# A transpose on TensorE that takes over the last addition of GpSimd

## The chip, the cores and the metric

The kernel runs on one core of a Trainium2 chip. Its engines work side by side, each through its own list of instructions, and wait for each other by semaphores: TensorE (PE; its weight loads are a row of their own, PEld), VectorE (DVE), ScalarE (ACT), GpSimd (POOL) and SyncE (SP), which starts transfers. The metric is the device time of one execution in microseconds, as the median over several.

## The reference

A GRU runs over 32 time steps on 32 sequences of 256 features; its states go through a feed-forward layer with a router, and the result is added to the input.

```python
def cell(h, x):                                   # 32 steps, one after the other
    gi = x @ W_ih + b_ih;  gh = h @ W_hh + b_hh   # [32, 768] each
    r = sigmoid(i_r + h_r);  z = sigmoid(i_z + h_z)
    n = tanh(i_n + r * h_n)
    h_new = (1.0 - z) * n + z * h

probs = softmax(xt @ w_router)                    # 1024 tokens, 128 experts
topk_p, topk_idx = top_k(probs, 4)
basis = silu(xt @ w_gate) * (xt @ w_up)           # [tokens, K=8, I=128]
mixed = einsum('tek,tki->tei', mix[topk_idx], basis)
out   = einsum('teh,te->th', mixed @ w_down, topk_w * expert_scale[topk_idx])
shared = silu(xt @ shared_w_gate) * (xt @ shared_w_up) @ shared_w_down
return x + out + shared
```

The kernel computes the routed part as one vector of 8 coefficients per token: the 8 basis blocks of 128 columns are scaled by them and added up to one block, which then goes through w_down.

## The kernel before, in words

The 1024 tokens are 8 chunks of 4 time steps by 32 sequences, 128 tokens each, one to a partition. Everything runs in the order in which it is written, engine by engine; no scheduler changes it.

**The recurrence.** In step t TensorE multiplies the state by W_hh (h_part, L619: 8 products of 32-column blocks of the array, which leave 16 records), ScalarE and VectorE apply the gates, and VectorE turns the new state (hT, L886). While they do so TensorE computes the input part of the next step (x_part, L583, 16 records) and then a piece of feed-forward work of a chunk that is complete: the filler. Before each filler piece stands what the order in filler(f) says, with k the step within a chunk, six steps behind the recurrence.

**The feed-forward work of chunk p.** k = 0: logits and unit 0 (a unit is 256 columns of gate and of up, each product of a token block by a weight in three reduced-precision parts, L640). k = 1: units 1 and 2, and project(p - 2). k = 2: the transpose of the expert mask (turn_em, L675), unit 3, and the coefficients (L681). k = 3: turn_hidden(p - 1) (L690 to L692), and unit 4. ScalarE and VectorE turn each unit into q, the basis, or shared.

**GpSimd.** In every step it first splits the new state into a high and a low part (halves: hThi L304, hTlo L306), for which it waits for hT. Behind that it does one piece of mixing: for k = 3 and k = 0 the scaling of q by the coefficients (qc, L316, 512 columns each), for k = 1 the addition of the two halves (half, L323), for k = 2 add_rest: 512 columns to 256 (quarter, L327), then 256 to 128 (mixed, L332). The semaphore pool_mix counts these operations, MIX_STEPS a chunk.

**The turn.** turn_hidden waits for pool_mix to reach the end of the chunk, and transposes mixed and the two blocks of shared into the bank turned, with ident as the moving operand. ScalarE (dhi, L485) and VectorE (dlo, L982) split it, and project (L702) multiplies by w_down two steps later.

**The tail.** After the last recurrent step the same work of the last chunks goes on without gate products, in an order of its own. The last chunk is scaled by ScalarE before it is added, so GpSimd only makes quarter from it (L380, L384); last_mixed_turned (L727) adds two parts of quarter and two blocks of q by four products with ident that accumulate in one bank. turn_hidden is so called seven times: for chunks 0 to 4 in the middle of the kernel, for chunk 5 in the tail's first part, for chunk 6 (LAST - 1) among the last chunk's units.

Of the kernel before, what the change touches and what calls it, by code (L numbers as in the profile page):

```python
# [29 lines left out]
ALU = mybir.AluOpType  # L30
# [3 lines left out]
P = 128  # L34
# [6 lines left out]
E, K, I = 128, 8, 128  # L41
# [19 lines left out]
def build(nc, x, cond, w_ih, w_hh, b_ih, b_hh, w_router, w_gate, w_up, w_down, amplitudes, expert_scale,  # L61
          sw_gate, sw_up, sw_down, out):
    with ExitStack() as ctx:
        def sb(name, shape, dt=F32):
            return ctx.enter_context(nc.sbuf_tensor(name, shape, dt))

        def bank(name):
            return ctx.enter_context(nc.psum_tensor(name, [P, 512], F32))

        def sem(name):  # L70
            return ctx.enter_context(nc.semaphore(name))
# [19 lines left out]
        ident = sb("ident", [P, P])  # L91
# [41 lines left out]
        qc = sb("qc", [P, K * I])  # L133
        half = sb("half", [P, 4 * I])
        quarter = sb("quarter", [P, 2 * I])
        mixed = sb("mixed", [P, I])
        dhi = sb("dhi", [P, 2, 3, P], F32R)
        dlo = sb("dlo", [P, 2, 3, P], F32R)
        ot = sb("ot", [P, 2, D])
# [4 lines left out]
        turned = bank("turned")  # L144
# [64 lines left out]
        pool_mix = sem("pool_mix")  # L209
        turned_ready = sem("turned_ready")  # L210
# [6 lines left out]
        stored = [sem("stored0"), sem("stored1")]  # L217

        TOPK_STEPS = 2
        MIX_STEPS = 5  # L220

        PIECES = [(u, s) for u in range(NU) for s in range(KB)]
        LO_VECTOR = sum(LO_VECTOR_AT, [])
# [1 line left out]
        LAST = NC - 1  # L225
# [59 lines left out]
        @block.gpsimd  # L285
        def _(pool):
            pool.wait_ge(zeroed, 2)
            pool.affine_select(out=pick4[:, :, :], in_=pick4[:, :, :], compare_op=ALU.not_equal, fill=1.0,
                               base=0, pattern=[[-1, NJ], [0, Q]], channel_multiplier=1).then_inc(const_ready, 1)
            pool.affine_select(out=ident[:, :], in_=ident[:, :], compare_op=ALU.not_equal, fill=1.0,  # L290
                               base=0, pattern=[[-1, P]], channel_multiplier=1).then_inc(const_ready, 1)
            pool.wait_ge(bias_ready, 1)
            pool.tensor_copy(early[:, :, HN:HN + FJ],
                             bias[:, HN:HN + FJ].rearrange("p (o c) -> p o c", o=1).to_broadcast([P, NE, FJ]))\
                .then_inc(early_hn, 1)

            def halves(t):

                c, k = t // TC, t % TC
                pool.wait_ge(hT_ready, t + 2)  # L300
                if k == 0 and c >= 3:

                    pool.wait_ge(unit_ready, NU * (c - 2))
                pool.tensor_copy(hThi[:, c % 3, :, :, k], hT[:, c % 2, :, k, :]).then_inc(hThi_ready, 1)  # L304
                pool.wait_ge(hThi_ready, t + 1)
                pool.tensor_tensor(hTlo[:, c % 3, :, :, k], hT[:, c % 2, :, k, :],  # L306
                                   hThi[:, c % 3, :, :, k].bitcast(F32), ALU.subtract).then_inc(hTlo_ready, 1)


            def scale_basis(p, part):  # L310

                if part == 0:
                    pool.wait_ge(coef_ready, p + 1)
                pool.wait_ge(q_ready, NU * p + 2 * (part + 1))
                ks, cols = slice(K // 2 * part, K // 2 * (part + 1)), slice(K // 2 * I * part, K // 2 * I * (part + 1))
                pool.tensor_tensor(qc[:, cols].rearrange("p (k i) -> p k i", i=I),  # L316
                                   q[:, p % 2, cols].rearrange("p (k i) -> p k i", i=I),
                                   coef[:, p % 2, ks].rearrange("p (k o) -> p k o", o=1).to_broadcast([P, K // 2, I]),
                                   ALU.mult).then_inc(pool_mix, 1)

            def add_half(p):
                pool.wait_ge(pool_mix, MIX_STEPS * p + 2)
                pool.tensor_tensor(half[:, :], qc[:, 0:4 * I], qc[:, 4 * I:8 * I], ALU.add).then_inc(pool_mix, 1)  # L323

            def add_rest(p):
                pool.wait_ge(pool_mix, MIX_STEPS * p + 3)
                pool.tensor_tensor(quarter[:, :], half[:, 0:2 * I], half[:, 2 * I:4 * I], ALU.add)\  # L327
                    .then_inc(pool_mix, 1)
                pool.wait_ge(pool_mix, MIX_STEPS * p + 4)
                if p >= 1:  # L330
                    pool.wait_ge(turned_ready, p)
                pool.tensor_tensor(mixed[:, :], quarter[:, 0:I], quarter[:, I:2 * I], ALU.add)\  # L332
                    .then_inc(pool_mix, 1)

            def lo_piece(i):

                u, s = PIECES[i]
                cols = slice(UW * u, UW * (u + 1))
                pool.wait_ge(w_hi, i + 2)
                for a in range(2):  # L340
                    last = pool.tensor_tensor(wlo[:, s, a, cols], wraw[:, s, a, cols], whi[:, s, a, cols].bitcast(F32),  # L341
                                              ALU.subtract)
                last.then_inc(w_lo_pool, 1)

            def lo_down():
                pool.wait_ge(w_hi, len(PIECES) + 2)
                for a in range(3):
                    last = pool.tensor_tensor(dlo_w[:, a, :], draw[:, a, :], dhi_w[:, a, :].bitcast(F32), ALU.subtract)
                last.then_inc(w_lo_pool, 1)

            def mixing(f):
                p, k = f // TC, f % TC
                if p >= 0 and k == 3:
                    scale_basis(p, 0)
                if p >= 1 and k == 0:
                    scale_basis(p - 1, 1)
                if p >= 1 and k == 1:
                    add_half(p - 1)
                if p >= 1 and k == 2:
                    add_rest(p - 1)  # L360

            for c in range(NC):
                for k in range(TC):
                    t = TC * c + k
                    halves(t)
                    if t < len(LO_POOL_AT):
                        for i in LO_POOL_AT[t]:
                            lo_piece(i)
                    if t == len(LO_POOL_AT):
                        lo_down()  # L370
                    mixing(t - TC - SKEW)
            for f in range(T - TC - SKEW, TC * LAST):
                mixing(f)
            scale_basis(LAST - 1, 1)
            add_half(LAST - 1)
            add_rest(LAST - 1)

            scaled = q[:, LAST % 2, :]
            pool.wait_ge(q_ready, NU * LAST + 3)
            pool.tensor_tensor(half[:, 0:2 * I], scaled[:, 0:2 * I], scaled[:, 2 * I:4 * I], ALU.add)\  # L380
                .then_inc(tail_mix, 1)
            pool.wait_ge(tail_mix, 1)
            pool.wait_ge(q_ready, NU * LAST + 4)
            pool.tensor_tensor(quarter[:, :], half[:, 0:2 * I], scaled[:, 4 * I:6 * I], ALU.add).then_inc(tail_mix, 1)  # L384

        @block.scalar
        def _(act):
# [77 lines left out]
            def scale_up(u):  # L465
# [3 lines left out]
                if u == 0:  # L469
                    act.wait_ge(coef_ready, NC)  # L470
                    act.wait_ge(pool_mix, MIX_STEPS * (LAST - 1) + 3)
                if u >= 2:
# [75 lines left out]
        def _(pe):  # L548
# [134 lines left out]
            def turn_hidden(p):  # L683
                pe.wait_ge(q_ready, NU * (p + 1))
                pe.wait_ge(pool_mix, MIX_STEPS * (p + 1))
                if p >= 1:
                    pe.wait_ge(dlo_ready, p)
                else:
                    pe.wait_ge(early_ready, NE // 2)
                pe.transpose(turned[:, 0:P], mixed[:, :], ident[:, :])  # L690
                pe.transpose(turned[:, P:2 * P], shared[:, p % 2, 0:P], ident[:, :])
                pe.transpose(turned[:, 2 * P:3 * P], shared[:, p % 2, P:2 * P], ident[:, :]).then_inc(turned_ready, 1)  # L692

# [108 lines left out]
            n = NU * LAST  # L802
# [7 lines left out]
            last_shared_turned()  # L810
            unit(n + 2, [1])
            turn_hidden(LAST - 1)
            unit(n + 3, range(KB))
            unit(n + 4, range(KB))
# [6 lines left out]
        def _(dve):  # L821
# [109 lines left out]
            def gated_q(n):  # L931
# [4 lines left out]
                if n % NU == 0 and p >= 2:  # L936
                    dve.wait_ge(pool_mix, MIX_STEPS * (p - 2) + 2)
                dst = q[:, p % 2, UW * u:UW * (u + 1)] if u < NU - 1 else shared[:, p % 2, :]
# [170 lines left out]
```

## Time and profile before

| | |
|---|---|
| median of 3 runs | 145.73 us (145.5 to 149.58) |
| the profiled execution | 146.3 us, its span 144.4 us |
| TensorE, matmul | 136.0 us busy (94% of the span), 1489 records |
| TensorE, weight loads | 98.3 us (68%) |
| VectorE | 104.5 us (72%) |
| ScalarE | 72.8 us (50%) |
| GpSimd | 67.9 us (47%) |
| granted TensorE clock | 1.0 of full speed |

The busy times are those of the profiled execution. A matmul's record overlaps the next one, since TensorE is pipelined: what an instruction costs is read from the distance of one start to the next, not from its duration. The profile lists a weight load (PEld) for every matmul record.

### The profile page before, as it was taken

How to read it: one execution, taken by the hardware profiler on the slowest of the kernel's cores; microseconds unless marked ns; L12 is line 12 of the kernel's file. 1: busy time of each engine (PE TensorE's matmuls, PEld its weight loads, DVE VectorE, ACT ScalarE, POOL GpSimd, SP SyncE). 2: the span in 40 equal slices, each digit the busy share in tenths (PEclk: the TensorE clock that was granted, in tenths of full speed). 3: DMA queues.
4: the chain of work that ended last, by engine and by line, in shares of the span. 5: the costliest groups of instructions: out<-in, count | busy, mean ns of one | idle time of the engine just before them, and what ended most of it. 6: DMA issues, size and time to landing. Idle time of an engine off the chain costs nothing.

```text
span 144.4 us, 4045 instructions
## 1 busy us (share of the span) xinstructions
PE 136.0 (94%) x1489; PEld 98.3 (68%) x1489; DVE 104.5 (72%) x388; ACT 72.8 (50%) x246; POOL 67.9 (47%) x123
## 2 busy tenths in 40 slices
PE   7999999999899999999999999999999999899981
PEld 5556677666466667767676767676767676688881
DVE  2206699999878887785878587768785878676661
ACT  0404764666746575455545554555455535433830
POOL 2301165666656455435544554455445544884030
PEclk9999999999999999999999999999999999999999
DMA  3986995000000000000100010001000100010102
GB/s 78 310 272 181 289 339 156 2 7 0 0 5 0 0 0 5 2 2 5 36 0 0 5 36 0 7 2 36 5 0 0 36 5 0 2 36 0 36 5 73
DMA packets 5859, 7.12 MB, mean 49 GB/s; under 512 B 976, under 2 KB 4304, under 8 KB 5840
## 3 DMA queue, kind: packets, MB, share of 16 engines
q1 hardware_dynamic: 5616, 6.83, 14.7%
q8 instruction: 12, 0.20, 0.6%
q10 hardware_dynamic: 224, 0.04, 0.1%
q14 instruction: 7, 0.06, 0.1%
HBM read 5.81 MB, written 1.05 MB: 48 GB/s over the span
## 4 chain that ended last, share of the span: by engine, by line
PE 71%; DVE 14%; DMA 5%; ACT 4%; issue 3%; SPq 2%; DVEq 0%
PE unit L640 36%; PE gates L619 14%; PE down L702 5%; PE gates L583 5%; DMA whh<-in_L_cond_W_hh_dram 5%; DVE wlo L899 3%; DVE early L853 2%; PE route L652 2%; ACT sc_add L423 2%; DVE sc_out L879 2%; PE turned L690 1%; DVE pre L870 1%; PE route L675 1%; PE unit L598 1%; DVE hT L886 1%
## 5 line engine op out<-in xcount | busy, mean ns | idle before, releaser
L304 POOL CAST hThi<-hT 128x64 fp32r<-128x64 f32 x32 | 10.7, 333 | 56.2 <-DVE hT L886 56.2
L640 PE MATMUL unit<-whi,hThi 128*128 128x512 f32 x80 | 34.2, 427 | 0.1
L640 PE MATMUL unit<-wlo,hThi 128*128 128x512 f32 x80 | 31.7, 396 | 0.0
L640 PE MATMUL unit<-whi,hTlo 128*128 128x512 f32 x80 | 31.5, 394 | 0.0
L619 PE MATMUL gates<-whh,hT 128*32 128x192 f32 x512 | 27.4, 332 | 1.6 <-DVE hT L886 1.2
L416 ACT ACTIVATE trz<-gates 128x128 f32<-128x128 f32 x32 | 8.8, 275 | 31.2 <-PE gates L619 31.2
L619 PEld LDWEIGHTS gates<-whh,hT 128*32 128x32 f32 x512 | 13.4, 109 | 11.6 <-issue 4.6
L879 DVE TENSOR_TENSOR_SCAN sc_out<-sc_mul,sc_add 128x128 f32<-128x128 f32 x32 | 13.8, 431 | 8.0 <-ACT sc_add L423 7.5
L640 PEld LDWEIGHTS unit<-whi,hThi 128*128 128x128 f32 x80 | 15.4, 192 | 5.0 <-issue 2.1
L640 PEld LDWEIGHTS unit<-wlo,hThi 128*128 128x128 f32 x80 | 15.0, 188 | 3.5
L927 DVE SCALAR_TENSOR_TENSOR p<-th,unit 128x256 f32<-128x256 f32 x40 | 15.9, 410 | 1.5 <-ACT th L444 1.5
L640 PEld LDWEIGHTS unit<-whi,hTlo 128*128 128x128 f32 x80 | 15.1, 189 | 2.2
L867 DVE SCALAR_TENSOR_TENSOR m<-trz,gates 128x64 f32<-128x64 f32 x32 | 6.9, 217 | 12.7 <-ACT trz L416 12.5
L423 ACT ACTIVATE sc_add<-pre 128x64 f32<-128x64 f32 x32 | 10.3, 323 | 10.8 <-DVE pre L870 10.8
L444 ACT ACTIVATE th<-unit 128x256 f32<-128x256 f32 x40 | 14.2, 370 | 2.0 <-PE unit L640 2.0
L316 POOL TENSOR_TENSOR qc<-q,coef 128x512 f32<-128x512 f32 x14 | 14.6, 1040 | 0.5 <-DVE q L939 0.5
L306 POOL TENSOR_TENSOR hTlo<-hT,hThi 128x64 fp32r<-128x64 f32 x32 | 11.6, 363 | 2.6
L583 PE MATMUL gates<-wih,xT 128*32 128x192 f32 x224 | 11.7, 327 | 0.0
L939 DVE SCALAR_TENSOR_TENSOR q<-p,unit 128x256 f32<-128x256 f32 x28 | 11.1, 416 | 0.4
L418 ACT ACTIVATE sc_mul<-trz 128x64 f32<-128x64 f32 x32 | 10.2, 320 | 1.0
L341 POOL TENSOR_TENSOR wlo<-wraw,whi 128x256 fp32r<-128x256 f32 x12 | 9.7, 832 | 0.0
L873 DVE SCALAR_TENSOR_TENSOR sc_add<-trz,hhalf 128x64 f32<-128x64 f32 x32 | 9.6, 301 | 0.0
(129 smaller groups left out, 239.1 us busy)
## 6 DMA issues: line engine op xcount, KB each, us to landing
xtok<-in_x_dram SPq DMA_DIRECT2D x8, 128.0 KB, 3.3
wraw<-in_L_ffn_w_gate_dram SPq DMA_DIRECT2D x2, 512.0 KB, 5.9
wraw<-in_L_ffn_w_up_dram SPq DMA_DIRECT2D x2, 512.0 KB, 6.9
out_dram<-ot SPq DMA_DIRECT2D x8, 128.0 KB, 2.1
wih<-in_L_cond_W_ih_dram SPq DMA_DIRECT2D x2, 384.0 KB, 4.1
whh<-in_L_cond_W_hh_dram SPq DMA_DIRECT2D x1, 512.0 KB, 6.7
whh<-in_L_cond_W_hh_dram SPq DMA_DIRECT2D x1, 256.0 KB, 5.3
wraw<-L_ffn_shared_w_gate_dram SPq DMA_DIRECT2D x1, 256.0 KB, 7.5
```

The costliest lines, as they stand in the source:

```text
L304: pool.tensor_copy(hThi[:, c % 3, :, :, k], hT[:, c % 2, :, k, :]).then_inc(hThi_ready, 1)
L306: pool.tensor_tensor(hTlo[:, c % 3, :, :, k], hT[:, c % 2, :, k, :], hThi[:, c % 3, :, :, k].bitcast(F32), ALU.subtract).then_inc(hTlo_rea ...
L316: pool.tensor_tensor(qc[:, cols].rearrange("p (k i) -> p k i", i=I), q[:, p % 2, cols].rearrange("p (k i) -> p k i", i=I), coef[:, p % 2, ...
L418: act.activation(by_block(sc_mul, 1), natural(trz, slice(FJ, 2 * FJ)), ACT.Copy, bias=0.5, scale=-0.5)\
L423: act.activation(by_block(sc_add, 0), natural(pre, slice(0, FJ)), ACT.Tanh).then_inc(n_ready, 1)
L444: act.activation(th[:, n % 2, :], unit_bank[n % NB][:, 0:UW], ACT.Tanh, scale=0.5)\
L583: pe.matmul(g[Q * j:Q * (j + 1), R:4 * FJ], x_block(t, s), wih[:, s, :].rearrange("p (g j c) -> p j g c", g=3, j=NJ)[:, j], start=False, s ...
L619: last = pe.matmul(g[Q * j:Q * (j + 1), HN:HN + 3 * FJ], st, whh[:, s, :].rearrange("p (g j c) -> p j g c", g=3, j=NJ)[:, j], start=False, ...
L640: last = pe.matmul(dst, st[:, p % 3, s, :, :].rearrange("p b t -> p (b t)"), w[:, s, :, cols], start=(s == 0 and n == 0), stop=(s == KB - ...
L879: dve.tensor_tensor_scan(sc_out[:, :, :].rearrange("p f a -> p (f a)"), sc_mul[:, :, :].rearrange("p f a -> p (f a)"), sc_add[:, :, :].rea ...
L927: dve.scalar_tensor_tensor(out=p1[:, n % 2, :], in0=th[:, n % 2, :], scalar=1.0, in1=unit_bank[n % NB][:, 0:UW], op0=ALU.add, op1=ALU.mult)\
L939: dve.scalar_tensor_tensor(out=dst, in0=p1[:, n % 2, :], scalar=0.5, in1=unit_bank[n % NB][:, UW:2 * UW], op0=ALU.mult, op1=ALU.mult).then ...
```

## The change

GpSimd's last addition of a chunk (mixed) is taken out, with its tile and its step of the semaphore (MIX_STEPS is 4, not 5). TensorE turns the two parts of quarter instead: two plain matrix products with ident as moving operand, of which the second accumulates on the first, take the place of one transpose. The wait of GpSimd for the previous turn, which kept mixed from being overwritten, stands before the addition that writes quarter; the tail's writes to half and quarter get a wait each.

```diff
-        MIX_STEPS = 5
+        MIX_STEPS = 4
...
             def add_rest(p):
                 pool.wait_ge(pool_mix, MIX_STEPS * p + 3)
-                pool.tensor_tensor(quarter[:, :], half[:, 0:2 * I], half[:, 2 * I:4 * I], ALU.add)\
-                    .then_inc(pool_mix, 1)
-                pool.wait_ge(pool_mix, MIX_STEPS * p + 4)
                 if p >= 1:
                     pool.wait_ge(turned_ready, p)
-                pool.tensor_tensor(mixed[:, :], quarter[:, 0:I], quarter[:, I:2 * I], ALU.add)\
+                pool.tensor_tensor(quarter[:, :], half[:, 0:2 * I], half[:, 2 * I:4 * I], ALU.add)\
                     .then_inc(pool_mix, 1)
...
             scaled = q[:, LAST % 2, :]
+            pool.wait_ge(pool_mix, MIX_STEPS * LAST)
             pool.wait_ge(q_ready, NU * LAST + 3)
             pool.tensor_tensor(half[:, 0:2 * I], scaled[:, 0:2 * I], scaled[:, 2 * I:4 * I], ALU.add)\
                 .then_inc(tail_mix, 1)
             pool.wait_ge(tail_mix, 1)
+            pool.wait_ge(turned_ready, LAST + 1)
             pool.wait_ge(q_ready, NU * LAST + 4)
...
-                pe.transpose(turned[:, 0:P], mixed[:, :], ident[:, :])
+                for n in range(2):
+                    pe.matmul(turned[:, 0:P], quarter[:, I * n:I * (n + 1)], ident[:, :], start=(n == 0), stop=(n == 1))
                 pe.transpose(turned[:, P:2 * P], shared[:, p % 2, 0:P], ident[:, :])
```

## Rows read from the trace of the kernel before

**Rows 1.** The page: engines with busy us; granted TensorE clock by slices.
```profile
PE 136.0 (94%) x1489; PEld 98.3 (68%) x1489; DVE 104.5 (72%) x388; ACT 72.8 (50%) x246; POOL 67.9 (47%) x123
...
PEclk9999999999999999999999999999999999999999
```

**Rows 2.** The page: the chain that ended last, by engine and by line.
```profile
PE 71%; DVE 14%; DMA 5%; ACT 4%; issue 3%; SPq 2%; DVEq 0%
```

**Rows 3.** Busy time by windows, one chunk's period: PE, PEld, DVE, ACT, POOL.
```profile
85.35:99.85 14.50, 14.23 (x145) 10.39 (x146) 11.22 (x45) 7.74 (x29) 7.06 (x13) 1.00 0.03 11
```

**Rows 4.** Waits of the weight loads: releaser, us in total, times, longest.
```profile
PEld turned L690 <- issue: 3.8, 6, 0.7
...
PEld route L675 <- issue: 1.8, 6, 0.3
```

**Rows 5.** Timeline of the weight loads around a turn: start us, us, engine, line.
```profile
84.09 0.62 PEld L583 LDWEIGHTS gates<-wih,xT 128*32 128x32 f32 x16
85.32 0.14 PEld L690 LDWEIGHTS turned<-ident,mixed 128*128 128x128 f32 x1 [0.61 <-issue]
85.38 0.14 PEld L691 LDWEIGHTS turned<-ident,shared 128*128 128x128 f32 x1
...
85.60 0.19 PEld L640 LDWEIGHTS unit<-whi,hThi 128*128 128x128 f32 x1
...
87.19 0.48 PEld L619 LDWEIGHTS gates<-whh,hT 128*32 128x32 f32 x16 [0.36 <-issue]
```

**Rows 6.** Timeline of GpSimd in the same stretch.
```profile
83.99 0.72 POOL L327 TENSOR_TENSOR quarter<-half 128x256 f32<-128x256 f32 x1
84.80 0.46 POOL L332 TENSOR_TENSOR mixed<-quarter 128x128 f32<-128x128 f32 x1
86.50 0.30 POOL L304 CAST hThi<-hT 128x64 fp32r<-128x64 f32 x1 [1.25 <-DVE hT L886]
```

**Rows 7.** Timeline of the weight loads around the sixth turn, in the tail.
```profile
126.39 0.14 PEld L690 LDWEIGHTS turned<-ident,mixed 128*128 128x128 f32 x1 [0.70 <-issue]
...
126.68 0.19 PEld L640 LDWEIGHTS unit<-whi,hThi 128*128 128x128 f32 x1
```

**Rows 8.** Timeline of GpSimd in the tail: before the sixth turn and the seventh.
```profile
125.06 0.73 POOL L327 TENSOR_TENSOR quarter<-half 128x256 f32<-128x256 f32 x1
125.87 0.45 POOL L332 TENSOR_TENSOR mixed<-quarter 128x128 f32<-128x128 f32 x1
...
131.17 0.46 POOL L332 TENSOR_TENSOR mixed<-quarter 128x128 f32<-128x128 f32 x1
```

**Rows 9.** Timeline of the weight loads: the first of the seventh turn.
```profile
134.15 0.14 PEld L690 LDWEIGHTS turned<-ident,mixed 128*128 128x128 f32 x1
```

**Rows 10.** Timeline of the weight loads after gate products, in two other steps.
```profile
91.51 0.19 PEld L640 LDWEIGHTS unit<-whi,hThi 128*128 128x128 f32 x1 [0.30 <-issue]
91.62 0.19 PEld L640 LDWEIGHTS unit<-whi,hTlo 128*128 128x128 f32 x1
...
95.38 0.62 PEld L583 LDWEIGHTS gates<-wih,xT 128*32 128x32 f32 x16
96.30 0.14 PEld L675 LDWEIGHTS route<-ident,em 128*128 128x128 f32 x1 [0.30 <-issue]
```

**Rows 11.** Timeline of VectorE: the expert mask of the same chunk.
```profile
94.23 0.28 DVE L967 SCALAR_TENSOR_TENSOR em<-marked,ex 128x128 f32<-128x128 f32 x1
```

**Rows 12.** Groups of matmuls by line and shape: xcount, busy us, mean ns.
```profile
L690 PE MATMUL turned<-ident,mixed 128*128 128x128 f32 x7 | 2.1, 296 | 2.0 <-issue 2.0
...
L727 PE MATMUL gates<-ident,quarter 128*128 128x128 f32 x4 | 0.6, 274 | 0.0
```

**Rows 13.** Timeline of the weight loads of the tail's last turn.
```profile
139.19 0.53 PEld L727 LDWEIGHTS gates<-ident,quarter 128*128 128x128 f32 x4
139.64 0.53 PEld L727 LDWEIGHTS gates<-ident,q 128*128 128x128 f32 x4
```

**Rows 14.** Timeline of GpSimd: the tail's second addition.
```profile
138.34 0.74 POOL L384 TENSOR_TENSOR quarter<-half,q 128x256 f32<-128x256 f32 x1 [0.58 <-DVE q L947]
```

## What the change should do, predicted from these rows

> **What bounds the kernel.** I read the engine table and the slices first, then the chain that ended last, then one chunk's period, and at last the timelines of TensorE's weight loads and of GpSimd side by side around the lines that change.
>
> TensorE is busy 94% of the span and at the full granted clock (2.4 GHz) throughout [rows 1]. The chain runs over TensorE for 71% of the span; the rest lies in the first 40 us and at the very end [rows 2]. In the middle a chunk repeats every 14.50 us with TensorE busy 14.23 us of it [rows 3]. So from about 41 us on what counts is TensorE's stream, and the reader should ask of every edit: does it lengthen that stream, or does it shorten a hole in it?
>
> There is a hole exactly at the changed line. TensorE's weight loads stood idle 3.8 us over 6 times before the turn (L690), "issue" by the waits [rows 4], that is, the profile names no releaser. The timeline does. In the chunk shown, GpSimd's last addition (mixed) starts at 84.80 and takes 0.46, so ends at 85.26; the load of the turn starts at 85.32 [rows 5, 6]. The two follow each other by 0.06 us. In the tail it is the same: mixed ends at 125.87 + 0.45 = 126.32, the load comes at 126.39 [rows 7, 8]. And at the seventh turn, where mixed was done at 131.63, the load (134.15) follows its predecessors with no idle time [rows 8, 9]. TensorE waits for mixed at six turns of seven.
>
> **How much of that wait is real.** This is the step where one can go wrong. In the chunk shown, the load idles 0.61 us and comes 1.23 us after the first load of the input products (84.09) [rows 5]; at 56.32, 70.82, 99.82 and 114.32 it is alike. But a hole belongs there anyway: one step earlier the turn of the expert mask (L675), whose data had been ready for over a microsecond (em is written at 94.23 + 0.28 = 94.51 [rows 11]), comes 0.92 us after the first of the same sixteen loads, with 0.30 idle [rows 10]; it does so 6 times [rows 4], and a unit right behind gate products shows the same 0.30 [rows 10]. So going from 32-column products to a full array costs 0.30 us by itself, and mixed costs only 1.23 - 0.92 = 0.31 us of TensorE's time. With it gone the load can start at 84.09 + 0.92 = 85.01.
>
> **The change, part by part.**
>
> *The addition on GpSimd goes.* 7 x 0.46 = 3.2 us of GpSimd's time [rows 6, 8]. By itself worth nothing: after it GpSimd waits over a microsecond for the next hidden state [rows 6]. What counts is that the turn now waits for quarter, whose addition starts at 83.99 and takes 0.72 [rows 6]: ready at 84.71, and with 0.06 of signalling a load could start at 84.77. That is 0.24 before the natural 85.01, so in the five steady chunks the whole wait of 0.31 goes and GpSimd is no longer what sets the turn. What is late next is TensorE's own switch to the full array.
>
> *One transpose becomes two products.* A transpose is one record; the program's seven turns give seven [rows 12]. A plain f32 product is two records: the tail's last turn does the very same thing as the new code (quarter parts against ident) and its two products of quarter left four [rows 12]. The four loads take from 139.19 to 139.64, so 0.1125 each [rows 13]. Transposes of 128 columns follow each other at 0.11 as well (85.38 to 85.60 for two [rows 5]); the spacing is that of the weight loads in both. Four slots in place of one: 3 x 0.1125 = 0.34 us more on TensorE, seven times.
>
> *First load.* After the 32-column products the first transpose load is followed by the second after 0.06 us, but a first plain load by its second after 0.11 [rows 5, 10]. So 0.05 more in the five steady chunks. Put as positions: before, the unit's first load stood at 85.60 [rows 5]; now six slots of 0.112 after 85.01 give 85.68. Each steady chunk gets 0.08 us longer (-0.31 + 0.34 + 0.05), five of them 0.40.
>
> *The sixth turn*, in the tail, has no gate products before it. Quarter starts at 125.06 and takes 0.73, ends 125.79; the load can come at 125.85 instead of 126.39. The unit's load then comes at 125.85 + 0.67 = 126.52 instead of 126.68 [rows 7, 8]: 0.16 us gained.
>
> *The seventh turn* waited for nothing, so it pays in full: +0.34. From there to the last product TensorE's stream is unbroken, and the chain runs in it [rows 2], so this arrives at the end.
>
> *The waits that moved.* GpSimd now waits for the previous turn (turned_ready) before quarter, not before mixed. That turn lies 14.5 us back, so nothing; the instruction queued behind it is only the next split of the hidden state. The tail's second addition now waits for the seventh turn, over by 135 us, while it starts at 138.34, when its data come [rows 14]. The four loads there start at 139.19 [rows 13], just after its end at 139.08, and both sides shift by the same 0.34, since the units that feed them come after the seventh turn. No DMA is moved.
>
> *What hides nothing, and what still has room.* The hidden state arrives at GpSimd at 86.50, the gate products that need it start loading at 87.19 [rows 5, 6]: 0.7 us of room in that step, so 0.08 up or down triggers no wait of the recurrence. The copy of the turned tile (L485) runs two steps before its use.
>
> **Sum.** 5 x 0.08 - 0.16 + 0.34 = **+0.58 us**. The profiled execution took 146.3 us (span 144.4, so 1.9 around it), and would take 146.9. The median of the runs shown is 145.73; on it, **146.3 us**. A measurement of this kernel can tell about 2% (2.9 us) from no change, so this is "the same".
>
> A rule that speaks against the change: the Trainium skill, "TensorE: Matmul & The Clock Gate", Terms, calls the transpose mode four times faster for FP32 than the plain product, and "Perfetto Trace Analysis", Transposes, says to use a transpose and not a standard matmul for a logical transpose. By rows the two products take four slots for one, so one product is twice a transpose, not four times: both are held at the pace of the loads. By the page's figure the pair would take eight slots, and the sum would be +3.7; that is rival D.
>
> **The rivals.**
>
> *B: the whole wait was mixed.* If the 0.92 us is not a floor for this turn (the turn of the mask might have something of its own), its load comes at 84.77, 0.55 earlier, for 0.39 more work: -0.16 in each of five chunks, -0.16 for the sixth, +0.34 for the seventh: -0.62, 145.1 us. Against it: the same 0.30 before two different lines, a transpose and a plain product [rows 10]. Chance 0.18.
>
> *C: nothing of the wait is regained.* The gap stays 1.23 because TensorE's queue, not mixed, makes it, as the word "issue" says; the match with mixed's end would be chance. Then 6 x 0.39 + 0.34 = +2.7: 148.4 us. Against it: mixed's end meets the load within 0.07 at both kinds of place, with different distances to the work before. Chance 0.12.
>
> *D: the plain products cost twice the rows.* The place is L690 again; the mechanism: a product streams its 128 columns more often than the two records of the tail show, and fills four slots each instead of two. Every turn gets 4 x 0.1125 = 0.45 longer, 7 x 0.45 = 3.15 over my sum, +3.7: 149.5 us, slower by over 2%. It decides from (2.9 - 0.58) / 7 = 0.33 us more per turn on, so from a pair that takes 0.78 instead of 0.45. Against it: the loads of the tail are the same operation at full clock [rows 13]. Chance 0.06.
>
> *E: it doesn't do what it says*, the turn still waiting for GpSimd although one addition less stands there (quarter ready after 85.01). It would be late by at most what the split of the hidden state before it slips; +0.1 us per chunk, 146.8. Chance 0.04.
>
> My case has the remaining 0.60, with its own range 145.8 to 146.9 (the steady term between -0.02 and +0.18 a chunk). **Range:** D and C are left out (0.18), all else taken in: 145.0 to 147.7. **Chances:** slower by over 2% is D, 0.06; faster by over 2% (below 142.8) needs 3 us where all the waits at this line are 3.8 [rows 4] and 5 x 0.30 of them are the floor: 0.02; within 2%: 0.92.
>
> **What would show each step.** The first load of the turn 0.92 us after the first input load (C: 1.23; B: 0.68). Between it and the unit's first load 0.67 us (D: over 1.1). Period of the middle chunks 14.58 (B 14.34, C 14.89). Four records of L690's successor per turn, at 0.11. GpSimd's quarter ending 0.3 us ahead of that load. Span 145.0. I am wrong if the period gets shorter, or if the gate products are found to wait for the hidden state where they did not.

## The result, and the profile after

| | before | after |
|---|---|---|
| median of 7 runs each | 146.12 us (145.46 to 149.58) | 146.5 us (146.1 to 149.73) |
| ratio to before, 95% interval | | 1.0042 [1.0024, 1.006], so 0.6 us slower |
| profiled execution, its span | 146.3, 144.4 us | 146.1, 144.3 us |

Some executions of every kernel take about 3 us longer and are left out of the ratios; the profiled ones of experiments 1 to 4 are such, and there the 3 us lie in the first 14 us. So I compare profiles from one position behind them: the first input load (L583, after the change L581) of the step with the first turn, to the span's end.

The page of the changed kernel, engines with their busy time, answers to [rows 1]:

```profile
PE 138.1 (96%) x1510; PEld 100.6 (70%) x1510; DVE 104.6 (72%) x388; ACT 72.9 (51%) x246; POOL 64.7 (45%) x116
```

TensorE has 21 records more, 7 x 3, and GpSimd 7 fewer. The weight loads of the same chunk as in [rows 5], in the timeline of the changed kernel:

```profile
83.51 0.62 PEld L581 LDWEIGHTS gates<-wih,xT 128*32 128x32 f32 x16
84.43 0.52 PEld L689 LDWEIGHTS turned<-ident,quarter 128*128 128x128 f32 x4 [0.30 <-issue]
84.87 0.14 PEld L690 LDWEIGHTS turned<-ident,shared 128*128 128x128 f32 x1
84.98 0.15 PEld L691 LDWEIGHTS turned<-ident,shared 128*128 128x128 f32 x1
85.09 0.19 PEld L638 LDWEIGHTS unit<-whi,hThi 128*128 128x128 f32 x1
...
86.70 0.48 PEld L617 LDWEIGHTS gates<-whh,hT 128*32 128x32 f32 x16 [0.36 <-issue]
```

And GpSimd beside it, answering to [rows 6]:

```profile
83.40 0.75 POOL L328 TENSOR_TENSOR quarter<-half 128x256 f32<-128x256 f32 x1
85.93 0.30 POOL L303 CAST hThi<-hT 128x64 fp32r<-128x64 f32 x1 [1.78 <-DVE hT L885]
```

The turn's first load now comes 0.92 us after the first input load (before 1.23), with the 0.30 idle that the expert mask's turn also has [rows 10]. Quarter was done at 84.15, 0.28 ahead of it. From there to the unit's first load it takes 0.66 us (before 0.28): four slots of 0.11 in place of one, and 0.05 because the second load now follows the first by 0.11 and not by 0.06. The whole is 1.58 instead of 1.51.

What the 0.30 is can be seen in the row of the matmuls. Before the change, at the turn of mixed and at the turn of the expert mask:

```profile
84.25 0.83 PE L583 MATMUL gates<-wih,xT 128*32 128x192 f32 x16
85.35 0.30 PE L690 MATMUL turned<-ident,mixed 128*128 128x128 f32 x1 [0.27 <-issue]
...
95.54 0.83 PE L583 MATMUL gates<-wih,xT 128*32 128x192 f32 x16
96.30 0.33 PE L675 MATMUL route<-ident,em 128*128 128x128 f32 x1
```

And at the turn after the change:

```profile
83.67 0.83 PE L581 MATMUL gates<-wih,xT 128*32 128x192 f32 x16
84.43 0.71 PE L689 MATMUL turned<-ident,quarter 128*128 128x128 f32 x4
```

At the mask the input products run until 96.37 by this row, whose ends are modelled, and the next product starts at 96.30: the loads were idle for 0.30 us, the matmuls not at all. At the turn of mixed the matmuls stood still for 0.27 us, and after the change they don't (84.50, against 84.43). So in the 0.30 no weights are loaded while products are still under way, and the part of the wait that was mixed's own shows in this row by itself, 0.27 beside the 0.31 of the prediction. Over the whole chunk: the first input load of this step stands at 54.34, 68.92, 83.51, 98.10 and 112.70, a period of 14.59 us against 14.50.

The sixth turn and the seventh, the weight loads of the changed kernel, answering to [rows 7, 9]:

```profile
124.97 0.42 PEld L679 LDWEIGHTS route<-mix,emT 128*128 128x128 f32 x2
125.56 0.52 PEld L689 LDWEIGHTS turned<-ident,quarter 128*128 128x128 f32 x4 [0.17 <-issue]
...
126.22 0.19 PEld L638 LDWEIGHTS unit<-whi,hThi 128*128 128x128 f32 x1
...
133.14 0.19 PEld L638 LDWEIGHTS unit<-whi,hThi 128*128 128x128 f32 x1
...
133.73 0.65 PEld L689 LDWEIGHTS turned<-ident,quarter 128*128 128x128 f32 x4
...
134.52 0.19 PEld L638 LDWEIGHTS unit<-whi,hThi 128*128 128x128 f32 x1
```

From the fifth step's input load (112.70, before 113.09) to the unit's first load behind the sixth turn is 13.52 us, before 13.59 (126.68 - 113.09). That is 0.07 less, although the fifth turn itself takes 0.07 to 0.09 more, so the sixth gained 0.14 to 0.16. Quarter ended at 125.49 (124.76 + 0.73), 0.07 before that turn's first load, so here GpSimd still sets the turn. The seventh turn took 0.79 from its first load to the unit's (134.52 - 133.73), before 0.45 (134.60 - 134.15): it cost 0.34. The stretch from the sixth turn's unit to the seventh's took 8.30 against 7.92 (134.60 - 126.68), so 0.04 more was lost among the units between. From the first turn's input load to the end: 144.3 - 54.34 = 89.96 us, before 144.4 - 55.09 = 89.31. That is 0.65 us more, and the ratio says 0.6. The spans alone (144.3 and 144.4) hide it, since in this execution the head was done 0.75 us sooner: with the change the second group of bias products began at 4.94, before at 5.21, and the first gate products at 9.37, before at 10.03, where the matmuls had stood idle 0.32 us for the last transfer of W_hh.

### The profile page after: what moved, and what is told of

Same layout as the page of the kernel before. It is cut to its first block, busy times and chain, and to the rows that moved or that the text cites. A ratio compares the mean times of both kernels' runs of the same rounds, so it can differ in the third digit from the quotient of the medians.

```text
span 144.3 us, 4081 instructions
## 1 busy us (share of the span) xinstructions
PE 138.1 (96%) x1510; PEld 100.6 (70%) x1510; DVE 104.6 (72%) x388; ACT 72.9 (51%) x246; POOL 64.7 (45%) x116
## 4 chain that ended last, share of the span: by engine, by line
PE 79%; DVE 14%; ACT 4%; issue 1%; DVEq 0%
PE unit L638 36%; PE gates L617 14%; PE gates L581 6%; PE down L701 5%; PE turned L772 3%; PE turned L689 3%; DVE wlo L898 3%; DVE early L852 2%; PE route L650 2%; ACT sc_add L421 2%; DVE sc_out L878 2%; DVE pre L869 1%; PE route L673 1%; PE unit L596 1%; DVE hT L885 1%
## 5 line engine op out<-in xcount | busy, mean ns | idle before, releaser
L581 PE MATMUL gates<-wih,xT 128*32 128x192 f32 x224 | 11.7, 327 | 0.0
```

The lines of the kernel that those rows point to most:

```text
L581: pe.matmul(g[Q * j:Q * (j + 1), R:4 * FJ], x_block(t, s), wih[:, s, :].rearrange("p (g j c) -> p j g c", g=3, j=NJ)[:, j], start=False, s ...
```

## Experiments

All were timed against the kernel before. The ratios of experiments 2 and 4 rest on two executions each of the edited kernel.

**1. The GpSimd part alone.**

```diff
# the changed kernel, with
-                for n in range(2):
-                    pe.matmul(turned[:, 0:P], quarter[:, I * n:I * (n + 1)], ident[:, :], start=(n == 0), stop=(n == 1))
+                pe.transpose(turned[:, 0:P], quarter[:, 0:I], ident[:, :])
```

> The GpSimd part of the change alone: its last addition is gone, the turn waits for quarter, and TensorE turns the first part of quarter by one transpose as before. The second part is left out of the sum, so the kernel computes less. Theory A (a floor of 0.92 us from the first input load to the first load of a full array, behind it only 0.31 us of wait): the first turn load comes 0.92 us after the first input load, five steady chunks 0.31 us shorter each (period 14.19), the sixth turn 0.54 earlier, the seventh unchanged: 5 x 0.31 + 0.54 = 2.1 us less than before, ratio 0.986. Rival B (no floor, the whole wait was mixed): the load 0.68 us after the input load, 5 x 0.55 + 0.54 = 3.3 us less. Rival C (TensorE's queue makes the gap, not mixed): the load still 1.23 us behind, the time unchanged.

Ratio 0.9837 [0.9801, 0.9873], 2.4 us less. Its weight loads in one steady chunk:

```profile
100.89 0.62 PEld L581 LDWEIGHTS gates<-wih,xT 128*32 128x32 f32 x16
101.81 0.14 PEld L688 LDWEIGHTS turned<-ident,quarter 128*128 128x128 f32 x1 [0.30 <-issue]
101.87 0.14 PEld L689 LDWEIGHTS turned<-ident,shared 128*128 128x128 f32 x1
...
102.09 0.19 PEld L638 LDWEIGHTS unit<-whi,hThi 128*128 128x128 f32 x1
```

The load at 0.92, the unit's at 1.20 where it was at 1.51: 0.31, as theory A had it. Period 14.20 us. B's 0.68 and C's 1.23 are both refuted: the addition cost TensorE 0.31 us a chunk, neither its whole 0.46 (or the 0.55 until a load could come) nor nothing.

**2. The TensorE part alone.**

```diff
-                pe.transpose(turned[:, 0:P], mixed[:, :], ident[:, :])
+                for n in range(2):
+                    pe.matmul(turned[:, 0:P], mixed[:, :], ident[:, :], start=(n == 0), stop=(n == 1))
```

> The TensorE part alone: GpSimd still makes mixed, and the turn adds mixed twice by two accumulating products with ident in place of the transpose (so the routed part counts twice). Theory A: nothing is regained, four load slots for one cost 0.34 at each of seven turns, 0.05 more for the first plain load after 32-column products in five: 5 x 0.39 + 2 x 0.34 = 2.6 us more than before, ratio 1.018; the load stays 1.23 us behind the first input load. Rival D (a product fills four slots, not two): 5.8 us more. Together with the GpSimd part alone (-2.1) theory A gives the change's own +0.6; if the two don't add up to it, a part of the price is hidden by something else.

Ratio 1.0168 [1.0139, 1.0197], 2.4 us more. Its weight loads:

```profile
102.83 0.62 PEld L583 LDWEIGHTS gates<-wih,xT 128*32 128x32 f32 x16
104.07 0.52 PEld L691 LDWEIGHTS turned<-ident,mixed 128*128 128x128 f32 x4 [0.62 <-issue]
104.51 0.14 PEld L692 LDWEIGHTS turned<-ident,shared 128*128 128x128 f32 x1
104.62 0.14 PEld L693 LDWEIGHTS turned<-ident,shared 128*128 128x128 f32 x1
104.73 0.19 PEld L640 LDWEIGHTS unit<-whi,hThi 128*128 128x128 f32 x1
```

The load still waits until 1.24, and the unit follows at 1.90 in place of 1.51: the 0.39 of the sum. Period 14.90. The two parts add up: 14.20 + 14.90 - 14.50 = 14.60, and the whole change has 14.59.

**3. One product in place of two.**

```diff
# the changed kernel, with
-                for n in range(2):
-                    pe.matmul(turned[:, 0:P], quarter[:, I * n:I * (n + 1)], ident[:, :], start=(n == 0), stop=(n == 1))
+                pe.matmul(turned[:, 0:P], quarter[:, 0:I], ident[:, :], start=True, stop=True)
```

> The changed kernel with one plain product of the first part of quarter instead of two; the second part is left out of the sum. It isolates the price of one product: two load slots of 0.1125 fewer at each of seven turns, 1.6 us less than the change, so 1.0 us less than before (ratio 0.993), and 1.1 more than the GpSimd part alone, which has a transpose there (7 x 0.11 and 5 x 0.05). Rival D: 3.2 us less than the change.

Ratio 0.9915 [0.9876, 0.9954], 1.2 us less than before. One steady chunk:

```profile
101.24 0.62 PEld L581 LDWEIGHTS gates<-wih,xT 128*32 128x32 f32 x16
102.16 0.30 PEld L688 LDWEIGHTS turned<-ident,quarter 128*128 128x128 f32 x2 [0.30 <-issue]
...
102.60 0.19 PEld L638 LDWEIGHTS unit<-whi,hThi 128*128 128x128 f32 x1
```

Two loads, 0.44 us to the unit; with a transpose it is 0.28, with two products 0.66. So one product costs 0.16 more than a transpose here: one more load of 0.11, and 0.05 since its second load follows by 0.11 where a transpose's follower comes after 0.06. The second product costs 0.22. Period 14.36, against 14.20 in experiment 1. Rival D, four slots a product, is refuted.

**4. The turn behind the unit**, in the kernel before:

```diff
                     if k == 3:
-                        if p >= 1:
-                            turn_hidden(p - 1)
                         unit(NU * p + 4, range(KB))
+                        if p >= 1:
+                            turn_hidden(p - 1)
```

> The kernel before with one thing moved: in the step k = 3 TensorE does unit 4 first and turns mixed after it, so that the addition on GpSimd has 1.4 us more. Six turns of seven are moved. Theory A: the wait of 0.31 goes in five chunks, the gap of 0.30 now stands before unit 4's first load (0.92 after the first input load), its first plain load gives back 0.05; at the sixth turn about 0.7 goes: 5 x 0.26 + 0.7 = 2.0 us less than before, ratio 0.986. Rival B: the gap disappears for the turn and the unit needs none: 3.3 less. Rival C: no gain, since the queue's gap stays wherever the turn stands. A third outcome: the copy of the turned tile on ScalarE, which now comes late in the step, delays the next gates and takes the gain back: then TensorE's gate products wait for the hidden state.

Ratio 0.9834 [0.9811, 0.9858], 2.4 us less than before: the best kernel of this study, with the arithmetic of the kernel before. Its weight loads:

```profile
86.56 0.62 PEld L583 LDWEIGHTS gates<-wih,xT 128*32 128x32 f32 x16
87.48 0.19 PEld L640 LDWEIGHTS unit<-whi,hThi 128*128 128x128 f32 x1 [0.30 <-issue]
...
88.75 0.14 PEld L690 LDWEIGHTS turned<-ident,mixed 128*128 128x128 f32 x1
...
89.40 0.48 PEld L619 LDWEIGHTS gates<-whh,hT 128*32 128x32 f32 x16 [0.17 <-issue]
```

Mixed was done at 87.73 (87.27 + 0.46), the turn wants it at 88.75. The 0.92 with its 0.30 idle now belongs to the unit: it goes with whatever full-array load comes first behind the 32-column products. ScalarE shows how near the third outcome was:

```profile
89.51 0.49 ACT L485 ACTIVATE dhi<-turned 128x384 fp32r<-128x384 f32 x1 [0.56 <-PE turned L692]
90.33 0.28 ACT L416 ACTIVATE trz<-gates 128x128 f32<-128x128 f32 x1 [0.33 <-PE gates L619]
```

The copy ends at 90.00 and the next gates come at 90.33, so it delays nothing. Period 14.26 (14.25 to 14.27): 0.24 less, and 0.06 over the 14.20 of experiment 1, where the wait is gone and the turn stands in its old place.

**5. The change and the moved turn together** (the same edit in the changed kernel).

> The change and the moved turn together: GpSimd makes quarter alone, TensorE does unit 4 first and then adds and turns by two products. In the moved turn without the change the steady period was 14.27 us. Theory A: nothing of the addition on GpSimd is waited for any more, so taking it out gives nothing, and the products cost their 0.34 in full: period 14.61, 2.4 us more than the moved turn alone, 0.4 more than before (ratio 1.003), about the same as the change. Rival: GpSimd's 0.46 us a chunk is still worth something in another place (its other work, or VectorE beside it): then the period stays nearer to 14.27.

Ratio 1.0016 [0.9994, 1.0038]. Period 14.58, 0.32 over the moved turn alone. Once the addition is not waited for, taking it away is worth nothing, and the products cost about the 0.34 that was forecast: 1.0016 - 0.9834 = 0.018, or 2.6 us given away against experiment 4 (2.3 by the profiles below).

**6. Mixed last in the turn**, in the kernel before:

```diff
-                pe.wait_ge(pool_mix, MIX_STEPS * (p + 1))
...
-                pe.transpose(turned[:, 0:P], mixed[:, :], ident[:, :])
                 pe.transpose(turned[:, P:2 * P], shared[:, p % 2, 0:P], ident[:, :])
-                pe.transpose(turned[:, 2 * P:3 * P], shared[:, p % 2, P:2 * P], ident[:, :]).then_inc(turned_ready, 1)
+                pe.transpose(turned[:, 2 * P:3 * P], shared[:, p % 2, P:2 * P], ident[:, :])
+                pe.wait_ge(pool_mix, MIX_STEPS * (p + 1))
+                pe.transpose(turned[:, 0:P], mixed[:, :], ident[:, :]).then_inc(turned_ready, 1)
```

> The kernel before with the turn in another order: the two blocks of shared first, then the wait for GpSimd and mixed. Theory A: the shared loads come 0.92 and 0.98 us after the first input load, mixed's still at 1.23, when GpSimd is done, and the unit's first load 0.11 behind, at 1.34 in place of 1.51: 0.17 less in five steady chunks (period 14.33) and at the sixth turn, nothing at the seventh, 1.0 us less than before (ratio 0.993). If mixed's load moves ahead of 1.23, mixed was not what it waited for; if the unit's load doesn't move, the two transposes were not free to fill the wait.

Ratio 0.9897 [0.9856, 0.9938], 1.5 us less. A steady chunk and the sixth turn:

```profile
83.36 0.62 PEld L583 LDWEIGHTS gates<-wih,xT 128*32 128x32 f32 x16
84.29 0.14 PEld L689 LDWEIGHTS turned<-ident,shared 128*128 128x128 f32 x1 [0.30 <-issue]
...
84.59 0.14 PEld L692 LDWEIGHTS turned<-ident,mixed 128*128 128x128 f32 x1
...
124.34 0.14 PEld L690 LDWEIGHTS turned<-ident,shared 128*128 128x128 f32 x1
125.05 0.14 PEld L692 LDWEIGHTS turned<-ident,mixed 128*128 128x128 f32 x1 [0.57 <-POOL mixed L332]
```

Mixed's load is pinned at 1.23, as GpSimd sets it, while the shared loads move to 0.93 and fill the wait. The unit's first load came at 1.23 too, right with mixed's, where 1.34 was expected. And now the profile itself names GpSimd as releaser (0.57 at the sixth turn), for the wait that it had booked as "issue" [rows 4, 7]; the wait for pool_mix now stands alone before its transpose, while before it stood among three, which is the likely reason and was not tested by itself. The mean period is 14.30 against the expected 14.33.

**All together**, from the first turn's input load to the end of the span, each against the 89.31 us of before:

| kernel | us | measured | expected | by the ratio of the runs |
|---|---|---|---|---|
| the change | 144.3 - 54.34 = 89.96 | +0.65 | +0.58 | +0.6 |
| GpSimd part alone | 145.6 - 58.26 = 87.34 | -1.97 | -2.1 | -2.4 |
| TensorE part alone | 150.2 - 58.13 = 92.07 | +2.76 | +2.6 | +2.4 |
| one product | 146.5 - 58.16 = 88.34 | -0.97 | -1.0 | -1.2 |
| turn after unit | 145.4 - 58.04 = 87.36 | -1.95 | -2.0 | -2.4 |
| change, turn after unit | 144.1 - 54.40 = 89.70 | +0.39 | +0.4 | +0.2 |
| mixed last | 142.9 - 54.78 = 88.12 | -1.19 | -1.0 | -1.5 |

The ratios stand 0.2 to 0.5 us lower than the profiles in all experiments. Their intervals are 0.3 to 0.6 us wide to each side, so all but one take in the profile's figure (turn after unit misses by 0.1 us); what makes this small common shift stays open. It touches no comparison between the kernels.

## Why the prediction was right

**The floor under the wait** was the step that decided. The load at 0.92 was read off another line of the same kernel and came out at 0.92, after the change and in experiment 1. Rival B, which took the whole distance for the wait, would have forecast a gain; C, which believed the word "issue", 2.7 us of loss. The floor is right as a position, but the prediction's words that the step to the full array "costs 0.30 us by itself" say too much: it is the loads that idle, while the matmuls' row has no gap (95.54 to 96.37, the next from 96.30). By the starts, the next product comes 0.25 us after the last of the sixteen; how much of that is a cost of the step, and how much the last products' own time, no run here separates. The sum needed only the position.

**The price of the products** was right: 0.66 us to the unit's load against 0.67. So the pair takes four loads of 0.11, as much as four transposes. An estimate from the factor of four that the Trainium skill gives for FP32 ("TensorE: Matmul & The Clock Gate", Terms) was eight slots for the pair, and this trace does not agree with it. What the Trainium skill says in "Perfetto Trace Analysis", Transposes, to transpose with a transpose and not with a standard matmul, holds here in its direction: 0.28 us to the unit's load in experiment 1, 0.44 in experiment 3.

**The sum** of +0.58 met +0.65. The steady chunks gave 0.09 each for 0.08, the sixth turn gained 0.14 to 0.16 for 0.16, and the seventh cost 0.34 for 0.34. The 0.04 lost among the units before the seventh came back behind it (134.52 to 139.07, before 134.60 to 139.19). The ratio's interval, 0.35 to 0.88 us more, has the +0.58 in it and neither B's -0.62 nor C's +2.7 nor D's +3.7. One sign did not come: the span was to be 145.0 and was 144.3, because the head of this execution was 0.75 us shorter; no run shows the change to be the cause of that. And the upper end of the prediction's own range, +0.18 a chunk, gives 146.8 by its sum, not 146.9.

**The waits that were moved** cost nothing, as costed: quarter starts right behind hTlo as before, and the tail's second addition (138.20) waits for VectorE's data, not for the turn. The recurrence kept its room: the state reached GpSimd at 85.93, the gate products started to load at 86.70, 0.77 ahead.

**What the prediction did not see** is that its own reading named a better edit. It had TensorE waiting 0.31 us for an addition, with 1.4 us of a unit right behind that needed nothing from it. Moving the turn wins 0.24 of it a chunk and takes no work to do so; the change wins the whole 0.31 and pays 0.39.

## What to carry to other kernels

Before work goes to the engine that bounds the kernel to shorten a wait of it, find out how much of the idle time the wait makes: look for the same switch of work elsewhere in the trace, where nothing is waited for, and subtract it. Where it is the weight loads that idle, look at the matmuls' row beside them too. Here 0.61 us of idle loading held 0.31 of wait, less than the 0.39 that the cure cost, and the matmuls had idled 0.27. And first try to put independent work of the same engine into the wait; only the order of two calls had to change.

## What the runs showed of the hardware

- From products on 32-column blocks to the full array the weight loads idle 0.30 us, whoever comes first: a transpose (experiment 1), a plain product (experiment 3), a unit (experiment 4). The first full-array load comes 0.92 us after the first of the sixteen input loads in all of them. In the meantime the matmuls go on: at the mask's turn in the kernel before, the next one starts at 96.30, 0.07 us before the recorded end of the last 32-column product.
- Behind that step, a transpose's load is followed by the next one after 0.06 us (101.81 and 101.87 in experiment 1), the load of a unit's plain product by the next after 0.11 (91.51 and 91.62 [rows 10]).
- In these streams a plain f32 product that streams 128 columns takes two loads of 0.11 us, and a transpose one (experiments 3 and 1, and the tail's last turn [rows 13]).
